# Attention stage on one core: far columns turned in transposing mode, and a step's weighing moved behind its turning

## What is computed

```python
k = jnp.concatenate([k_img, k_word], axis=1)      # one image key and value ahead of the S words
v = jnp.concatenate([v_img, v_word], axis=1)
scores = jnp.einsum('bhqd,bhkd->bhqk', q, k) / jnp.sqrt(jnp.float32(HDIM))    # 16 heads of 32
causal = kj <= qi + 1
scores = jnp.where(causal[None, None], scores, jnp.float32(MASK_OUT))         # -10000, not -inf
scores = scores + mask
attn = jax.nn.softmax(scores, axis=-1)
out = jnp.einsum('bhqk,bhkd->bhqd', attn, v)
out = out.transpose(0, 2, 1, 3).reshape(B, S, EMBED)
out = out @ c_proj_w + c_proj_b
```

## Time and profile before

| | |
|---|---|
| median of 3 runs | 3945.68 us (3940.99 to 3946.48) |
| the profiled execution, its own time | 3943.71 us |
| its span in the trace | 3942.0 us |
| TensorE matmul busy | 3842.5 us (97%) |
| TensorE weight loads busy | 2541.7 us (64%) |
| VectorE busy | 2347.1 us (60%) |
| ScalarE busy | 1104.0 us (28%) |
| GpSimd busy | 48.1 us (1%) |
| mean granted clock of TensorE | 0.99 |

### The profile page before, as it was taken

How to read it: one execution, slowest core, us unless ns; L and a number is a source line. 1 busy time by engine, 2 the same in 40 slices (tenths; PEclk the granted TensorE clock), 3 DMA queues, 4 the chain that set the end, 5 groups by cost and what they waited for, 6 DMA issues and landing times. The chain is left out here.

```text
span 3942.0 us, 171610 instructions
## 1 busy us (share of the span) xinstructions
PE 3842.5 (97%) x78004; PEld 2541.7 (64%) x78004; DVE 2347.1 (60%) x8864; ACT 1104.0 (28%) x3961; POOL 48.1 (1%) x277
## 2 busy tenths in 40 slices
PE   7999999999999999999999999999779999999998
PEld 5776667677767677777676777676435555555555
DVE  3566666666666666666666666666336566665664
ACT  2211111111111111111111111111106555555555
POOL 0000000000000000000000000000000000000000
PEclk9999999999999999999999999999979999999999
DMA  4100000000000000000000000000100000000000
GB/s 170 28 3 3 3 3 3 4 3 3 4 3 4 3 3 4 3 4 3 4 3 3 4 3 4 3 3 3 66 6 4 12 12 9 12 12 15 12 7 20
DMA packets 34254, 46.70 MB, mean 12 GB/s; under 512 B 5820, under 2 KB 22252, under 8 KB 33527
## 3 DMA queue, kind: packets, MB, share of 16 engines
q1 hardware_dynamic: 31222, 29.43, 2.4%
q10 hardware_dynamic: 2304, 6.29, 0.4%
HBM read 27.33 MB, written 8.39 MB: 9 GB/s over the span
## 5 line engine op out<-in xcount | busy, mean ns | idle before, releaser
L189 PE MATMUL bank<-wh,h 128*16 128x256 f32 (+1 forms) x16960 | 990.2, 374 | 32.4 <-ACT h L238 32.4
L167 PE MATMUL bank<-wh,h 128*8 128x256 f32 x16352 | 976.1, 379 | 9.1 <-DVE h L361 9.1
L189 PEld LDWEIGHTS bank<-wh,h 128*16 128x16 f32 (+1 forms) x16960 | 491.1, 97 | 341.3 <-ACT h L238 46.0
L167 PEld LDWEIGHTS bank<-wh,h 128*8 128x8 f32 x16352 | 444.8, 90 | 345.9 <-DVE h L361 20.1
L333 DVE STREAM_TRANSPOSE tp<-bank 128x256 f32<-128x256 f32 x512 | 230.3, 450 | 606.7 <-PE bank L167 605.1
L173 PE MATMUL bank<-wh,h 128*8 128x128 f32 x16352 | 540.0, 273 | 0.0
L173 PEld LDWEIGHTS bank<-wh,h 128*8 128x8 f32 x16352 | 447.1, 90 | 108.2
L243 ACT ACTIVATE gates_sb<-pre_sb 128x32 f32<-128x32 f32 x512 | 117.5, 229 | 1207.1 <-DVE pre_sb L335 1207.1
L208 PE MATMUL bank<-first,w_qkv 128*32 128x128 f32 x11904 | 393.2, 273 | 0.0
L208 PEld LDWEIGHTS bank<-first,w_qkv 128*32 128x32 f32 x11904 | 339.9, 110 | 64.3
L238 ACT ACTIVATE h<-sum 128x64 f32<-128x64 f32 (+1 forms) x530 | 135.1, 255 | 782.0 <-DVE sum L285 782.0
(11 more groups left out here) (139 smaller groups left out, 3241.1 us busy)
## 6 DMA issues: line engine op xcount, KB each, us to landing
xrows<-in_x_dram SPq DMA_DIRECT2D x32, 256.0 KB, 3.0
out_dram<-X SPq DMA_DIRECT2D x32, 256.0 KB, 2.6
w_qkv<-in_L_cond_c_attn_w_dram SPq DMA_DIRECT2D x1, 3072.0 KB, 17.0
w_qkv<-in_L_cond_w_W_dram ACTq DMA_DIRECT2D x4, 512.0 KB, 7.7
wh<-in_L_cond_w_W_dram ACTq DMA_DIRECT2D x4, 512.0 KB, 13.7
wx<-in_L_cond_Wx_dram SPq DMA_DIRECT2D x2, 1024.0 KB, 7.4
wh<-in_L_cond_Wh_dram SPq DMA_DIRECT2D x2, 1024.0 KB, 9.4
mask_all<-in_mask_Bx1x1xS_ff_dram SPq DMA_DIRECT2D x8, 256.0 KB, 3.5
```

The source lines that it names most:

```text
L167: mm = pe.matmul(mem.ps0[32 * j:32 * j + B, 0:2 * P], state[:, k, :], columns_of(mem.wh0[:, k, 0:3:2, :], j), start=(k == 0), stop=(k == K ...
L189: mm = pe.matmul(mem.ps12[32 * j:32 * j + B * len(ls), P * l0:P * l1], h12[:, k, (n - 1) % HR, l0:l1, :].rearrange("p l b -> p (l b)"), co ...
```

## The change

Three edits. (1) The extra columns are brought over with `pe.transpose` instead of a matmul against the identity, and come out in partitions 0 to 7 of the bank for every query tile, where they stood at partition 32 x qc before. (2) ScalarE's copy L858 therefore reads partitions 0 to 7; it still writes partitions 32 x qc on. (3) The call of weigh stands at the end of the step, behind the second part of turn and the second product.

```diff
@@ turn, last group
                         pe.transpose(bank[:, P:2 * P], mem.shares[:, v % RING, :], mem.ident[:, :])
-                        mm = pe.matmul(bank[FAR * qc:FAR * qc + EXTRAS * HPG, 0:P],
-                                       mem.extras[:, v % RING, :], mem.ident[:, :], start=True, stop=True,
-                                       skip_group_check=True)
+                        mm = pe.transpose(bank[0:EXTRAS * HPG, 0:P], mem.extras[:, v % RING, :], mem.ident[:, :])
@@ the loop over steps
-                if i >= 3:
-                    weigh(i - 3)
                 if 2 <= i < UNITS + 2:
                     turn(i - 2, 2, None)
                 for job in jobs[1:]:
                     product(*job)
+                if i >= 3:
+                    weigh(i - 3)
@@ ScalarE, keep_turn
-                        nc.scalar.copy(mem.probs_extra[rows, qc, :], bank[rows, 0:P])
+                        nc.scalar.copy(mem.probs_extra[rows, qc, :], bank[0:EXTRAS * HPG, 0:P])
```

## The result

The changed kernel took 3896.54 us (median of 4, 3894.76 to 3897.95) beside 3945.7 for the kernel before (median of 4, 3940.99 to 3946.48): a ratio of 0.9878, 95% interval 0.9861 to 0.9895. It is faster, by 49 us; I had forecast 3908, 37.7 less, with a range that ended at 3901, so the gain was larger than the range allowed. In two later measurements the changed kernel had medians of 3900.63 and 3901.17, on either side of that end.

What follows compares the result with a forecast made beforehand. TensorE's own work and its seams were taken to bound the kernel. Savings 30.8 + 3.2 + 0.7 + 1.6 = 36.3 took the profiled 3943.71 to 3907.4, given as 3908 us after the run median; range 3901 to 3921.

Steps and rivals of the forecast that it cites:

- Bounds, and the way of reading: Attention, batches 1 to 6: TensorE busy 813.98 of 820.20 us sets the time; seams read from start-to-start distances.
- Seam behind the product, cold weights: Between product and first transposition: array-shape change, 0.10 saved; first transposition's late weight load, 0.05 saved per step.
- Extra columns in front of a weighing, one pass: L771 before the moved weighing: one transposing pass costing 0.09 without a seam behind; 0.23 saved per step.
- the full kinds: Attention steps other than 0 and 2, 6, 10, 14: 0.38 saved each, 81 steps, 30.8 us.
- the steps with image scores: Steps 2, 6, 10, 14, order kept: L771 loses one pass, 0.11 in 29 steps, 3.2 us.
- Rival (b): L771 runs as a whole-array transposition; 0.19 x 29 = 5.5 saved by two seams before image scores; 3902, chance 0.06.
- a threat to the pass: At L771, the skill's rule would mean no pass gained by the extra columns: 25.8 saved, 3918; chance 0.16.
- Step 0: Batches 1 to 7, second product waits some 0.15 for VectorE's copy; saving falls to 0.1, 0.7 us in all.
- Steps 1, 5, 9, 13: Turning five groups: shares' wait for ScalarE's third-group copy stays 0.4, nothing replaces it; 0.38 still saved per step.
- The end: Last weighings: the one before now lies in the last one's wait, 1.2 saved, and 0.4 at step 128.
- Rival (c), the clock: Packed turning, shares and extra columns behind the product bring clock falls costing 1.7 each; up to 4013, chance 0.04.
- at most one fall less: Lower end of the range, 3901: the whole-array transposition case with one clock fall less.

Runs made afterwards that it cites:

- the quarter product: Changed kernel with the last quarter of the product put between the fourth group and the shares in steps turning five groups: 3885.38 us, ratio 0.9844 to before.

## Why the prediction was wrong

**Bounds, and the way of reading.** Right. The attention was bound by TensorE, and by start-to-start distances. Of the other engines only two waits showed in batches 1 to 6: the 0.40 for ScalarE's copy in steps 1, 5, 9 and 13, before and after, and after the change the wait for VectorE's copy in step 0; both were in the prediction.

**Seam behind the product, cold weights.** Right to 0.01: L718 to L765 3.44 (forecast 3.43), four transpositions 0.43 (0.44).

**The extra columns: the first step that failed.** "Extra columns in front of a weighing, one pass", at 0.09 and in the weighing's shape, by the earlier trace rows. Those rows show the matmul. The transposition takes 0.11 and leaves the seam behind it: shares, extra columns and seam together 0.31, where I had 0.29. In the full kinds that is a small error (0.36 a step for 0.38, 1.7 us in 73 steps). In the steps with image scores it was the large one: I took off a pass, 0.11, where a pass, two seams and cold weights went, 0.40; 27 steps, 7.8 us short. Rival (b) named the shape, but its price had the same kind of hole: two seams, 0.19, and not the 0.11 of cold weights in the image scores. With those 0.11, and the 0.02 a step that the full kinds lose by the shape, its 3902 would have been some 3901. The Trainium skill, "TensorEngine Tiling (Array Packing)", Restrictions and Gotchas, says that column tiling and the transposing mode for float32 exclude each other; I read it as a threat to the pass. The rows agree with the sentence in another sense: the transposition takes its one pass, and has no seam to whole-array work.

**Step 0.** The sum was right, 0.10, and its parts were not: the second product could have begun 0.11 behind L771, as no seam stands there, and waited 0.35 for VectorE's copy; I had put a seam and a wait of 0.15 (0.12 by the prediction's own two times). The copy sets the start either way.

**Steps 1, 5, 9, 13.** Right: the wait stayed at 0.40, cause and size. ("0.93 + 0.06 unwaited" counted the cold weights twice, as the 0.93 holds them; 1.33 less 0.93 is the 0.4 that I used. The 0.06 comes behind the wait, when the shares load cold.) I said that nothing replaces it and stopped there; it was worth 13 to 14 us, as the quarter product showed.

**The end.** Forecast 1.6; 1.5 together with the last five steps, in which nothing was to be won.

**Rival (c), the clock.** Falls of the clock, 3.41 us each, in step 2 of batches 1 to 7 were two in before and two in its repeat, two in the changed kernel, one and three in its repeats. In batches 1 to 6 no other step had any, in any of the ten traces. The Trainium skill, "TensorE: Matmul & The Clock Gate", Part 4, says that transposing mode doesn't count as PE-busy "the same way"; by that the piece would look idler, and no more falls were seen for it.

**The time ahead of the attention: the second step that failed.** The range ended at 3901 since I gave the clock at most one fall less. The 6.1 us ahead of the attention were outside every case I had: I took "the scan is unchanged" to mean that its time is, and put the difference at nothing. The spread of the three runs shown, 5.5 us, was there to be used for it. (The later trace showed that such a spread comes from elsewhere than the attention, which took 999.24 and 999.26.)

In sum: forecast 36.3; plus 6.0 for the shape (7.8 less 1.7 and rounding), plus 6.1 of the clock, 48.4; the spans differ by 48.3. Either alone would have left the profiled time just inside the range, at 3901.4 or 3901.3. That the sum closes to 0.1 is partly luck: the changed kernel's attention had 4.2 us more at the lower clock, some 2.1 lost, and batch 0 and the end won about as much more than I had forecast. The 6.1 are luck of that execution too; the repeats of the changed kernel reached their first scores at 2940.6 and 2942.1.

## What to carry to other kernels

Where TensorE is busy all the time, count the changes of array shape in a step, by the distance from start to start: here each cost about 0.1 us and 0.05 to 0.1 more for the first weights behind it, and work of one shape put together saves them. Two edits that each remove a seam next to the same piece don't add up, and what an operation costs in one mode is no row for the other mode: price both shapes at every place where it stands. A wait that "goes along unchanged" is the next gain; look what independent work, or what part of it, could stand there.

## What was not expected of the hardware

A float32 transposition with 8 columns of weights behaved at its seams like work in the whole array's shape: 0.11 from a 128*128 transposition, 0.20 to 128*32 work; the matmul with the same weights and the same moving operand had it the other way round, 0.20 and 0.01. No transposition of the ten traces was nearer than 0.20 to the 128*32 work behind it, and twice in a row stood 0.11 apart. The trace does not show why.

Ten executions whose scans are the same program stood 20.5 to 51.2 us at the lower clock where the scan runs out, and reached the first scores between 2936.7 and 2945.4 us.
